# Two normalisations handed from GpSimd to Vector, function tables loaded ahead, and new orders on all engines, in a two-block Swin kernel

## The reference, cut to what matters

```python
h = _ln(x, ln1_g, ln1_b)                      # normalisation A
h = jnp.roll(h, (-3, -3), axis=(1, 2))        # then cut into 7 x 7 windows
qkv = h @ qkv_w + qkv_b
attn = softmax(q * scale @ k.T + rel_bias + attn_mask)
x = x + roll_back(attn @ v @ proj_w + proj_b)
m = _ln(x, ln2_g, ln2_b)                      # normalisation M
m = gelu(m @ fc1_w + fc1_b)                   # 96 -> 384
m = _ln(m, ln3_g, ln3_b)                      # block 0 only
x = x + m @ fc2_w + fc2_b                     # 384 -> 96
```

## Time and profile before

| | |
|---|---|
| median of 3 runs | 6766.94 us (6766.27 to 6767.63) |
| the profiled execution's own time | 6768.22 us |
| its span, first to last instruction | 6766.4 us |
| PE busy | 6490.4 us (96%) |
| PE weight loads busy | 5930.6 us (88%) |
| ACT busy | 5582.5 us (83%) |
| DVE busy | 5373.0 us (79%) |
| POOL busy | 4507.8 us (67%) |
| mean granted TensorE clock | 0.993 of full speed |

### The profile page before, as it was taken

The page is one execution under the profiler, slowest core; times in us unless marked ns, Lnnn a source line. Parts: engine busy times, 40 slices in busy tenths (PEclk is TensorE's granted clock), DMA queues, the critical chain, the costliest instruction groups (busy, mean ns, idle before and its releaser), DMA issues.

```text
span 6766.4 us, 288144 instructions
## 1 busy us (share of the span) xinstructions
PE 6490.4 (96%) x97836; PEld 5930.6 (88%) x97836; DVE 5373.0 (79%) x19245; ACT 5582.5 (83%) x11780; POOL 4507.8 (67%) x4612
## 2 busy tenths in 40 slices
PE   6999999999999999999999999999999999999999
PEld 5988888888888888888888888888888888888888
DVE  5878787878888888888888888888888888888786
ACT  4888888888888888888888888888888888888887
POOL 3666666666666666666666666666666666666665
PEclk8999999999999999999999999999999999999998
DMA  2111111111111111111111111111111111111111
GB/s 62 52 48 48 49 48 49 48 49 47 49 47 49 47 49 48 49 48 49 48 49 48 49 48 49 48 50 47 50 47 50 47 49 47 49 48 48 48 48 36
DMA packets 604535, 327.88 MB, mean 48 GB/s; under 512 B 449917, under 2 KB 603903, under 8 KB 604095
## 3 DMA queue, kind: packets, MB, share of 16 engines
q1 hardware_dynamic: 603992, 322.32, 18.2%
q10 hardware_dynamic: 486, 4.82, 0.2%
HBM read 82.89 MB, written 38.54 MB: 18 GB/s over the span
## 4 chain that ended last, share of the span: by engine, by line
PE 95%; ACT 3%; issue 1%; DVE 1%; SPq 0%; DMA 0%; POOL 0%; ACTq 0%; DVEq 0%; POOLq 0%
PE ps L402 21%; PE ps L553 16%; PE ps L499 12%; PE ps L466 9%; PE ps L417 9%; PE ps L420 7%; PE ps L418 7%; PE ps L445 6%; PE ps L523 6%; ACT hid L705 2%; PE ps L560 2%; SPq L294 0%; ACTq L635 0%; DMA wproj<-in_wproj 0%; PE ps L396 0%
## 5 line engine op out<-in xcount | busy, mean ns | idle before, releaser
L975 POOL TENSOR_TENSOR rstdA<-var_epsA,minus_half 98x4 f32<-98x4 f32 x512 | 519.1, 1014 | 1646.4 <-DVE var_epsA L843 1646.3
L874 DVE TENSOR_TENSOR shifted<-ps,negmax 113x392 f32<-113x392 f32 x2048 | 1160.9, 567 | 213.0 <-DVE negmax L870 0.5
L870 DVE TENSOR_REDUCE negmax<-ps 113x8 f32<-113x392 f32 x2048 | 1143.5, 558 | 200.3 <-PE ps L466 200.3
L688 ACT ACTIVATE probsT<-ps 98x392 f32<-98x392 f32 x2048 | 959.2, 494 | 341.7 <-PE ps L402 341.1
L681 ACT ACTIVATE probs<-shifted 113x392 f32<-113x392 f32 x2048 | 1048.8, 524 | 124.1 <-DVE shifted L874 120.5
L402 PE MATMUL ps<-ident,probs 113*98 113x113 f32 x8192 | 1075.4, 264 | 9.1 <-ACT probs L681 6.2
L673 ACT ACTIVATE ps<-table 113x392 f32 (+1 forms) x2048 | 937.5, 493 | 8.7 <-DVE x_mid L897 2.6
L499 PEld LDWEIGHTS ps<-vM,probsT 98*49 98x49 f32 x32768 | 816.3, 125 | 137.3 <-issue 73.7
L499 PE MATMUL ps<-vM,probsT 98*49 98x18 f32 (+1 forms) x32768 | 899.5, 202 | 0.1
L402 PEld LDWEIGHTS ps<-ident,probs 113*98 113x98 f32 x8192 | 824.3, 129 | 48.0 <-ACT probs L681 12.1
L705 ACT ACTIVATE hid<-ps,bfc 128x392 f32<-128x392 f32 x1536 | 793.9, 600 | 12.0 <-PE ps L420 8.8
(11 more groups left out here) (104 smaller groups left out, 15405.9 us busy)
## 6 DMA issues: line engine op xcount, KB each, us to landing
kM<-kT SPq DMA_DIRECT2D x512, 85.8 KB
vM<-vA SPq DMA_DIRECT2D x1024, 41.3 KB
vM<-vA SPq DMA_DIRECT2D x1024, 38.3 KB
x_in<-in_x SPq DMA_DIRECT2D x256, 147.0 KB
x_again<-in_x SPq DMA_DIRECT2D x256, 147.0 KB
kM<-kT SPq DMA_DIRECT2D x1024, 36.8 KB
x_keep<-x_next SPq DMA_DIRECT2D x256, 147.0 KB
out_y<-y_out SPq DMA_DIRECT2D x256, 147.0 KB
```

The costliest lines, as they stand in the source:

```text
L688: act.activation(probsT[:, unit_buffer(L, u), :, :, :], free(ps[bank_of[f"T{L}{u}"]][0:PT, 0:1], (SP, 4), (64, 2), (1, TOK)), ACT.Copy).th ...
L870: dve.tensor_reduce(negmax[:, buf, :], s, AX.X, ALU.max, negate=True).then_inc(s_mx[L], 1)
L874: dve.tensor_tensor(shifted[0:SP, buf, :].rearrange("p (h k) -> p h k", k=TOK), s, free(negmax[:, buf, 0:1], (1, 8), (0, TOK)), ALU.add).t ...
L975: pool.tensor_tensor(rstd[n][:, :], var_eps[n][:, :], minus_half[:, :], ALU.pow).then_inc(s_rstd[n], 1)
```

## The change

DVE gets a function `norm` of its own, four `tensor_scalar` operations over 98 x 96 (subtract the mean, multiply by the root, both read per partition), and uses it for M0 and M1. GpSimd keeps `norm` for A0 and A1 and keeps all four `inverse_root`. ACT gets `table_ahead`, a one-element activation of Gelu or Exp that carries the table load to another place: Gelu's to the first place of a turn, Exp's between the last seed and the first exps. The orders of all five engines and the banks are new, and some stages work on a strip one turn earlier.

```diff
+            def table_ahead(x, n):
+
+                if not x.known or x.i > 0:
+                    act.wait_ge(s_spark[n], x.count(1, 0))
+                act.activation(spark[n][:, :], ones[0:1, 0:1], {"Exp": ACT.Exp, "Gelu": ACT.Gelu}[n]).then_inc(s_spark[n], 1)
...
+            def norm(x, n):
+                if not x.exists(ns):
+                    return
+                if x.back().exists(ns):
+                    dve.wait_ge(s_xt[n], x.back().count(1, 1))
+                dve.wait_ge(s_rstd[n], x.count(1, 1))
+                for p in range(PAIRS):
+                    ins = dve.tensor_scalar(xn[n][:, p, :], SRC[n][:, p, :], mv[n][:, p, 0:1], rstd[n][:, p:p + 1],
+                                            ALU.subtract, ALU.mult)
+                ins.then_inc(s_xn[n], 1)
...
             def body(i):
-                s0, s3, s4, s5 = Strip(i, 0), Strip(i, 3), Strip(i, 4), Strip(i, 5)
-                inverse_root(s4, "A1")
-                norm(s4, "A1")
+                s0, s3, s5 = Strip(i, 0), Strip(i, 3), Strip(i, 5)
                 inverse_root(s3, "M0")
-                norm(s3, "M0")
+                add_bias(s3, 0)
+                inverse_root(s5, "M1")
+                squares(s3)
                 inverse_root(s0, "A0")
-                add_bias(s3, 0)
-                squares(s3)
                 norm(s0, "A0")
-                inverse_root(s5, "M1")
                 rstd_of_third(s3)
-                norm(s5, "M1")
+                inverse_root(s3, "A1")
+                norm(s3, "A1")
                 add_bias(s5, 1)
```

More of the change, by code:

```diff
@@ L140, in swin_program @@
         gate = sb("gate", [1, 1])
+        spark = {"Exp": sb("spark_exp", [1, 1]), "Gelu": sb("spark_gelu", [1, 1])}
         minus_half = sb("minus_half", [PT, PAIRS])
@@ L200, in swin_program @@
         s_s = pairsem("s_s")
+        s_spark = {n: sem("s_spark_" + n) for n in ("Exp", "Gelu")}
         s_ready = sem("s_ready")
@@ L564, in body @@
             def body(i):
[L565 to L587, removed]
+                s0, s1, s2, s3, s4, s5, s6 = Strip(i, 0), Strip(i, 1), Strip(i, 2), Strip(i, 3), Strip(i, 4), Strip(i, 5), Strip(i, 6)
                 k(s4, 1)
@@ L594, in body @@
                 fc1(s3, 0, 2)
[L595 removed]
+                k(s1, 0)
+                scores(s4, 1, (0, 1, 2))
                 fc2(s6, 1)
[L597 to L598 removed]
+                scores(s4, 1, (3, 4, 5))
+                fc2(s3, 0)
                 probs_turn(s2, 0, 0)
[L600 removed]
+                probs_turn(s4, 1, 0)
                 probs_turn(s2, 0, 1)
[L602 removed]
+                probs_turn(s4, 1, 1)
+                q(s1, 0)
                 attend(s2, 0, 0)
+                attend(s4, 1, 0)
                 attend(s2, 0, 1)
[L605 to L606 removed]
+                probs_turn(s4, 1, 2)
+                probs_turn(s4, 1, 3)
+                xT(s5, "M1")
+                v(s1, 0)
+                scores(s1, 0, (0, 1))
+                o_turn(s2, 0)
+                probs_turn(s4, 1, 4)
+                xT(s0, "A0")
+                probs_turn(s4, 1, 5)
+                project(s2, 0)
+                xT(s3, "A1")
+                attend(s4, 1, 1)
+                attend(s4, 1, 2)
+                attend(s4, 1, 3)
+                attend(s4, 1, 4)
+                attend(s4, 1, 5)
+                fc1(s5, 1, 0)
             iterate(pe, body)
@@ L708, in body @@
             def body(i):
[L709 to L727, removed]
+                s0, s1, s2, s3, s4, s5, s6 = Strip(i, 0), Strip(i, 1), Strip(i, 2), Strip(i, 3), Strip(i, 4), Strip(i, 5), Strip(i, 6)
+                table_ahead(Strip(i, 0), "Gelu")
                 gelu(s6, 1, 0)
-                turned(s1, "A0")
+                k_out(s4, 1)
@@ new lines, in body @@
+                exps(s2, 0, 1)
+                probsT_out(s2, 0, 0)
+                probsT_out(s4, 1, 0)
+                exps(s4, 1, 3)
+                probsT_out(s4, 1, 1)
+                probsT_out(s2, 0, 1)
+                q_out(s1, 0)
+                seed(s1, 0, 0)
+                exps(s4, 1, 4)
+                seed(s1, 0, 1)
+                turned(s5, "M1")
+                probsT_out(s4, 1, 2)
+                v_out(s1, 0)
+                probsT_out(s4, 1, 3)
+                exps(s4, 1, 5)
@@ L753, in _ @@
+                o_out(s2, 0)
+                probsT_out(s4, 1, 4)
+                turned(s0, "A0")
+                exps(s1, 0, 0)
+                probsT_out(s4, 1, 5)
+                turned(s3, "A1")
             iterate(act, body)
```

61 lines of the change are left out of this document (33 added, 28 removed), and 12 rows, old and new, of the table BANKS.

## The result

The changed kernel takes 7168.8 us (median of 4 executions, 7165.7 to 7170.1) against 6767.3 us (6766.3 to 6768.7) on the same chip: ratio 1.059, 95% interval 1.057 to 1.061. It is slower by 401 us; 6702 had been forecast, in a range up to 7090. What happened is the first rival, norm M1 running into the squares, and the time lies above the rival's 7084 us as well.

A forecast was written before the change was run, and what follows sets the result against it. PE was taken as the bound, with one wait a turn, 0.82 us for a Gelu; removing it and adding two new waits gave 6768 - 201 + 246 x (0.30 + 0.25) = 6702 us, range 6560 to 7090.

The forecast's parts named there:

- the first rival: Norm M1's fourth DVE operation blocked by GpSimd's squares, delaying PE's second scores 1.8 us a turn: 7084 us, chance 0.28.
- Step 1: Gelu table load runs ahead on ACT behind two copies; PE's whole k1 wait goes, gaining 201 us.
- Step 2: Four GpSimd operations fewer, eight DVE more: DVE from 20.9 to 22.4 of 25 us, fits as an average.
- p: Start-to-start time of DVE's new normalisation operations, taken as 0.18 us between bounds of 0.13 and 0.22.
- A: Reference time: PE's start of the stage behind project 1.
- Step 3: Norm M0's first DVE operation blocked by GpSimd's bias addition; new PE wait 0.3 us a turn, between 0.14 and 0.43.
- R: Reference time: start of residual 0, taken as 0.20 us after PE has left project 0.
- Step 4: PE waits for GpSimd's sum of squares, held by the last Gelu: 0.25 us a turn, between 0.1 and 0.45.
- Step 5: Moved DMAs: SP issues the same 18 transfers a turn, early enough, so they cost nothing.
- eight operations of the free-running kind: By the port rule, eight such operations became eight that can be blocked, which speaks against the change as drawn.

The follow-up runs named there:

- run 1: Kernel before with only the Gelu and Exp table loads moved ahead, orders, banks and GpSimd norms unchanged: 6510.0 us, ratio 0.962.
- run 12: Changed kernel without the two one-element activations that load the tables ahead: 7193.8 us, ratio 1.063.
- runs 6, 10, 11: Kernel before with loads ahead and norms on DVE in the old orders: both 6850.0 us, only M0 6751.9, only M1 6605.9.
- run 8: Changed kernel with DVE's residual 0 moved from the head of the loop body to the end of the previous turn's: 7121.5 us, ratio 1.052.
- run 3: Changed kernel with GpSimd's bias addition of block 0 moved behind the squares, ahead of the normalisation of A0: 7068.2 us, ratio 1.044.
- run 7: Changed kernel with one added wait: GpSimd starts the squares only after DVE has finished norm M1: 6925.3 us, ratio 1.023.
- run 9: Changed kernel with three edits together: squares wait for norm M1, bias 0 behind the squares, residual 0 at the body's end: 6901.0 us, ratio 1.020.
- run 4: Changed kernel with both moves: bias of block 0 later on GpSimd, norm M1 later on DVE, behind the shifts: 7065.0 us, ratio 1.043.

## Why the prediction was wrong, step by step

*What bounds the kernel.* PE, and its one wait: right. "PE without that wait needs 25.97 - 0.82 = 25.15": too much, it is 24.91 (run 1), since the wait cost 1.06 a turn.

*Step 1, the load ahead.* Right in kind, and the wait is gone. By the weight loads' row it should have been 251 us in the sum. But for the changed kernel this gain belongs to the orders and the load together: without the loads ahead after loses only 25 us (run 12).

*Step 2, the added operations.* This is the step that failed, twice. First the size: "I take p = 0.18" from bounds of 0.13 and 0.22; the operations start 0.24 us apart. The scalar_tensor_tensor with one scalar per partition, 0.22, was the nearer row, and even it was no upper bound. The first of norm M1 came at A + 3.74 (A is 3004.36 in the turn shown; forecast 3.65) and the squares at A + 4.33 (forecast 4.4). With 0.18 the fourth would have started at A + 4.28, 0.05 us before the squares. With 0.24 it started at A + 4.46. With the prediction's own start and squares, 0.24 gives A + 4.37, still 0.03 before the squares: the later start and the earlier squares, each inside 0.1 us, were needed too. Second, "DVE goes from 20.9 to 22.4 of 25 us. As an average this fits" costs the added work at nothing. It has no term in the sum, because an average showed room. In the old orders, where the norms meet no collision, they cost 340 us (runs 6, 10, 11), 1.34 us a turn, of which norm M0 alone is 0.96. They delay what stands behind them on DVE, and PE waits for that in a turn in which DVE as a whole still waits 2.19 us.

*Step 3, norm M0.* The mechanism is right: the first operation ends with the bias addition. The wait is 0.9 us, not 0.3, against an upper bound of 0.43. The parts: 3 x 0.06 = 0.18 from p, 0.26 from the late residual, and 0.10 from the bias, which ends at R + 4.10 and not 4.00; with the forecast 0.3 that is 0.84, and the rest, 0.06, wasn't traced. Moving the residual (run 8) gave only 0.07 of its 0.26 back at this place. Run 3 took 0.4 of it away and won 101 us.

*Step 4, the squares.* Not seen in after, since PE comes 1.65 us late to that point. When the collision is taken away it appears as 0.6 us (run 7), above its bounds of 0.1 to 0.45; there the squares also wait for norm M1.

*Step 5, the DMAs.* PE has no wait for a DMA in the steady turns of after: right.

*The first rival.* It named the place, the rule ("a fourth start later than A + 4.4") and the wait, 1.8 us against 1.65 measured. Its 7084 us fell short mostly because it took M0's wait from step 3. With the sizes measured the turn nearly closes: 24.91 + 0.9 + 1.65 = 27.46, against 27.49. That its number came within 85 us is in part luck: with step 1 at the 256 us of run 1 it would have said 7029. The collision's net price is shown by run 7, 244 us. Beside it stood what the prediction had no rival for: work put into DVE's row at a place where nothing absorbs it. Of the 659 us between after and the kernel with the loads alone, 197 go to the orders and 462 to the norms on DVE. Within the 462 us, taking away the collision with the squares gave 244 (run 7) and the bias at norm M0 101 (run 3). With the residual moved as well the three gave 268 in place of 392 (run 9), so these prices do not add. What the norms cost in the new orders with no collision wasn't measured.

The Trainium skill's rule in "SBUF — State Buffer", section "Who interferes with whom", weighed in the prediction, agrees with the new rows: the operation that met the squares took 2.15 us in place of 0.33, and ended 0.06 us behind them. The prediction's count beside it, eight operations of the free-running kind, is wrong: four GpSimd operations a turn went, and eight on DVE came.

## What to carry to other kernels

Don't take an engine's room from an average. DVE was busy 20.9 us a turn and occupied 22.2 by its waits, and by either figure 1.9 us more would have fitted; 1.34 of them went into the turn. Look for the wait that stands next behind the place of the new work: norm M1 had one and cost 0.37 us a turn, norm M0 had none and cost 0.96. In a row that is back to back, each operation put in delays all behind it, and another engine shows that as small waits for banks that name something else. Moving work on an engine that shares something with a second one moves collisions too: runs 4 and 9 each removed some and made new ones, so look at the lengths of the operations again after each edit. A margin of 0.2 us made of ten estimated durations decides nothing: four operations 0.06 us farther apart than assumed and two shifts of under 0.1 us turned it, and one wait that put GpSimd behind them gave 244 us back. An edit that is worth 256 us in one order was worth 25 in another, so measure it alone in the order that is to be kept.

## What the runs showed of the hardware

- A tensor_scalar of 98 x 96 in fp32 with two scalars per partition takes 0.32 to 0.33 us where GpSimd does not hold it, and four in a row start 0.24 us apart; the scalar_tensor_tensor of the same shape had 0.22.
- Such an operation that started during a GpSimd operation over 98 x 384 or 128 x 1176 ended 0.06 to 0.08 us behind it (2.15 and 0.70 us long in after, 0.83 in run 4).
- For the stall at k1, the wait of TensorE's weight loads was nearer to the cost than that of its matmuls: 251.0 us against 201.1, and 256 us were won when it went.
- The first instruction of a loop's body started 0.17 us later than the same instruction at the body's end (0.46 against 0.29 us behind the same matmuls).
- The one-element activation that loads a table takes 0.20 us behind the load of 1.28 us.
